# Moving the row-maximum reductions on VectorE and the loop boundary on TensorE in a masked graph attention kernel

## What is computed

```
xn = layernorm(x)
q, k, v = xn @ Wq, xn @ Wk, xn @ Wv            # 2 heads of 64
scores = (q * SCALE) @ k.T, -9e15 where adj == 0
attn = softmax(scores)
sat = attn @ v
out = concat(sat[:2048] @ weightr, sat[2048:] @ weightd) + bias
x = x + leaky_relu(out)
y = layernorm(x); the two best of 8 experts by y @ Wg + bg
x = x + sum over chosen experts of (gelu(y @ W1 + b1) @ W2 + b2)
```

## Time and profile before

| | |
|---|---|
| median of 3 runs | 804.45 us (804.39 to 804.54) |
| profiled execution | 804.59 us, its span 802.9 us |
| granted TensorE clock | 0.999 of full |
| busy: TensorE / its weight loads | 776.4 us (97%) / 576.5 us (72%) |
| busy: VectorE | 650.5 us (81%) |
| busy: ScalarE | 684.7 us (85%) |
| busy: GpSimd | 683.3 us (85%) |
| chain that ended last | PE 84%, POOL 5%, DVE 5%, issue 4% |
| L692, mask preparation, 64 times | 676 / 824 / 1725 ns (least, median, most) |
| L743, row maximum, 64 times | 156 / 157 / 158 ns |

### The profile page before, as it was taken

How to read it: one execution, slowest core, us unless ns; L and a number is a source line. 1 busy time by engine, 2 the same in 40 slices (tenths; PEclk the granted TensorE clock), 3 DMA queues, 4 the chain that set the end, 5 groups by cost and what they waited for, 6 DMA issues and landing times.

```text
span 802.9 us, 34579 instructions
## 1 busy us (share of the span) xinstructions
PE 776.4 (97%) x13088; PEld 576.5 (72%) x13088; DVE 650.5 (81%) x1470; ACT 684.7 (85%) x1099; POOL 683.3 (85%) x673
## 2 busy tenths in 40 slices
PE   4999999999999999999999999999998999999997
PEld 2467777777777777777777777777777677777775
DVE  7887999889889898989889888988985777545554
ACT  4678888888889888888888888888988999999996
POOL 4799999999999999999999999999986767667664
PEclk9999999999999999999999999999999999999999
DMA  9633533353344334343443335334200000000000
GB/s 230 119 61 61 86 64 66 61 85 59 59 64 79 59 65 68 63 72 59 70 73 61 63 61 85 59 59 65 53 1 2 2 14 16 15 15 13 13 13 13
DMA packets 40906, 45.02 MB, mean 56 GB/s; under 512 B 22168, under 2 KB 32160, under 8 KB 40864
## 3 DMA queue, kind: packets, MB, share of 16 engines
q0 software_dynamic: 9216, 33.56, 25.8%
q1 hardware_dynamic: 31216, 10.71, 5.7%
q10 hardware_dynamic: 432, 0.20, 0.1%
HBM read 71.72 MB, written 2.10 MB: 92 GB/s over the span
## 4 chain that ended last, share of the span: by engine, by line
PE 84%; POOL 5%; DVE 5%; issue 4%; ACT 1%; DMA 1%; DVEq 0%; POOLq 0%
PE ps L1074 18%; PE ps L1095 18%; PE ps L1128 13%; PE ps L1121 10%; PE ps L1253 4%; PE ps L1255 3%; PE ps L1254 3%; PE ps L1196 3%; PE ps L1197 3%; PE ps L1198 3%; PE ps L1139 2%; POOL w_pair L367 1%; DVE prob L735 1%; POOL pt_half L351 1%; PE ps L1147 1%
## 5 line engine op out<-in xcount | busy, mean ns | idle before, releaser
L735 DVE CUSTOM_DVE_ANT_0 prob<-ps,mask 128x1024 f32<-128x1024 f32 x256 | 310.5, 1219 | 40.9 <-PE ps L1074 38.8
L351 POOL TENSOR_TENSOR pt_half<-pt_raw,pt_half 128x512 f16<-128x512 f32 x252 | 302.8, 1222 | 10.5
L534 ACT ACTIVATE prob<-prob,nmax 128x1024 f32<-128x1024 f32 x256 | 292.9, 1144 | 0.1
L1095 PEld LDWEIGHTS ps<-ident,prob 64*128 64x128 f32 x4096 | 154.1, 138 | 66.1 <-issue 62.4
L1074 PE MATMUL ps<-k_half,q_row 64*128 64x512 f16 x1536 | 188.2, 376 | 1.2 <-DVE k_half L685 0.8
L1095 PE MATMUL ps<-ident,prob 64*128 64x64 f32 x4096 | 180.9, 227 | 6.8 <-ACT prob L534 2.0
L461 POOL TENSOR_TENSOR prob<-prob 128x512 f16<-128x512 f32 x104 | 123.8, 1194 | 56.9 <-ACT prob L612 53.9
L347 POOL TENSOR_SCALAR pt_half<-pt_raw 128x1024 f16<-128x1024 f32 x126 | 138.6, 1100 | 22.4 <-PE ps L1121 11.8
L1128 PE MATMUL ps<-pt,v_sb 128*64 128x128 f32 x2048 | 125.9, 276 | 0.0
L967 DVE SCALAR_TENSOR_TENSOR x_sb<-ps,k_half,x_sb 128x128 f32<-128x128 f32 (+1 forms) x256 | 72.1, 344 | 64.6 <-PE ps L1255 61.9
L1074 PEld LDWEIGHTS ps<-k_half,q_row 64*128 64x128 f16 x1536 | 73.8, 95 | 61.0 <-issue 9.7
(11 more groups left out here) (124 smaller groups left out, 1115.5 us busy)
## 6 DMA issues: line engine op xcount, KB each, us to landing
mask<-in_adj POOLq DMA_DIRECT2D x64, 512.0 KB, 5.4
q_row<-q_nat SPq DMA_DIRECT2D x128, 32.0 KB, 1.9
x_sb<-in_x SPq DMA_DIRECT2D x4, 512.0 KB, 7.0
out<-x_sb SPq DMA_DIRECT2D x8, 256.0 KB, 2.3
x2t_hi<-in_L_ffn_W SPq DMA_DIRECT2D x1, 1024.0 KB, 6.5
wq_sb<-in_L_gnn_Wq ACTq DMA_DIRECT2D x1, 64.0 KB, 2.8
wk_sb<-in_L_gnn_Wk ACTq DMA_DIRECT2D x1, 64.0 KB, 4.4
wv_sb<-in_L_gnn_Wv ACTq DMA_DIRECT2D x1, 64.0 KB, 5.6
```

Of the source, the lines that this page charges most:

```text
L351: ins = pool.tensor_tensor(pt_lo[:, q, part, :], pt_raw[:, q % 2, part, :], pt_hi[:, q, part, :], ALU.subtract)
L534: act.activation(prob[:, h, cols], prob[:, h, cols], ACT.Exp, bias=nmax[:, h:h + 1], scale=-1.0, accum_out=sums[:, j, h, p:p + 1]).then_in ...
L735: dve.tensor_tensor_reduce(out=prob[:, h, col_of(p)], in0=ps[:, 2 * (u % 2):2 * (u % 2) + 2, :].rearrange("p b c -> p (b c)"), in1=mask[:, ...
L1095: ins = pe.transpose(ps[:, bank + half, t * DH:(t + 1) * DH], prob[part, h, (p * KT + t) * P:(p * KT + t + 1) * P], ident[part, part])
```

## The change

The row maximum of head 0 is issued behind the mask preparation of unit 5, not ahead of it. The row maximum of head 1 leaves the end of its step: it is issued in the next step, behind the copy of unit 0 and ahead of the masking of unit 0. Tile 0 keeps its own place for it. On TensorE block 0 of step 4 is written out, the loop runs 13 times instead of 14 over blocks 1 to 3 of an even step, the odd step and block 0 of the next even step, and blocks 1 to 3 of step 30 and step 31 are written out behind it.

```diff
--- before.py
+++ after.py
@@ -42,6 +42,7 @@
 BOTH_HEADS = (2, 3, 6, 7)
 AV_BLOCK = 2
 LOOP_UNIT = 2
+LOOP_BLOCK = 1
 SPLIT_P = (1, 3)
 SPLIT_UNITS = (1, 3, 5, 7)
 NS = len(SPLIT_UNITS)
@@ -876,12 +877,16 @@
                         finish_tile(i - 2, par)
                     if prior and u in DVE_COPIES:
                         copy_pt(i - 1, u, early, last)
+                    if prior and u == 0 and not early:
+                        row_max(i - 1, 1, 7)
                     if now:
                         mask_scores(i, par, u, prior)
-                        if u in (5, 7):
-                            row_max(i, u // 7, u)
                     if ahead and u in (1, 5):
                         make_mask(i + 1, 1 - par, u // 4)
+                    if now and u == 5:
+                        row_max(i, 0, 5)
+                    if now and u == 7 and not prior:
+                        row_max(i, 1, 7)
                     if post and par == 1:
                         if u == 1:
                             invert_sums(i - 3)
@@ -1158,9 +1163,10 @@
                     ins = pe.matmul(scores_t, x2t_lo[:, rows], wg_pair[:, 0, :], start=False, stop=True)
                 ins.then_inc(logit_psum, PAIR)
 
-            def step(i, par, prior=True, now=True, drain=True, post=True, ready=True, early=False):
-
-                for k in range(NU // 2):
+            def step(i, par, prior=True, now=True, drain=True, post=True, ready=True, early=False,
+                     blocks=range(NU // 2)):
+
+                for k in blocks:
                     if prior:
                         transposes(i - 1, 2 * k, early, not now)
                     if now:
@@ -1203,7 +1209,13 @@
             step(2, 0, post=False)
             pe.wait_ge(small_split, SMALL_SPLITS)
             step(3, 1, ready=False)
-            pairs(pe, 4, NT, step)
+            step(4, 0, blocks=range(LOOP_BLOCK))
+            with pe.Fori(0, (NT - 4) // 2 - 1) as k:
+                step(2 * k + 4, 0, blocks=range(LOOP_BLOCK, NU // 2))
+                step(2 * k + 5, 1)
+                step(2 * k + 6, 0, blocks=range(LOOP_BLOCK))
+            step(NT - 2, 0, blocks=range(LOOP_BLOCK, NU // 2))
+            step(NT - 1, 1)
             step(NT, 0, now=False)
             attend(NT - 1, NP - 2)
             x2_transpose(NT - 2 * PAIR)
```

## The result

The changed kernel takes 800.74 us, the median of 6 runs (800.33 to 801.28), against 804.5 us of the kernel before (6 runs, 804.29 to 805.06). The ratio is 0.9948, its 95% interval 0.9938 to 0.9958. So it is faster by 3.8 us, where 7.9 were forecast, and 0.5 us outside the range of 794.8 to 800.2. The profiled execution took 801.28 us, at a granted clock of 0.999.

The account below looks back on a forecast made before the run. TensorE, busy 97%, was taken as the bound. Gaps of 0.24 + 0.18 + 0.22 + 0.04 = 0.68 us over twelve pairs give 8.2, plus about 0.3, less 0.4: net 8.1, so 796.6 us, range 794.8 to 800.2.

Parts of the forecast that it names:

- Rivals A and B: A: port stays lost, 0.22 us gaps stay, 799.2, 10%; B: block 0 comes back only by half, 799.1, 11%.
- Rival D: Slower: unit 2's transposes wait for ScalarE's late copy of unit 1 in every row; 808.3 with no cover, 5%.
- part 3: TensorE's loop turned by one block: ahead of the even step 0.04 us comes back and 0.07 stays.
- the three other gaps: Block 0 of even and odd steps, and ahead of the odd step: 0.24, 0.18 and 0.22 us to come back.
- the fourth gap: TensorE's gap ahead of the even step, 0.11 us over: 0.04 us to come back, 0.07 to stay.
- part 1: Head 1's maximum moved: block 0 regains 0.24 and 0.18 us; ScalarE's unit 1 copy ends at about its old time.
- Rival E: No change: GpSimd becomes the period, its 0.91 us idle against 0.68 a pair asked back; about 804.5, 5%.
- The range: Forecast time between 794.8 (all 0.75 us a pair back) and 800.2 us, taking in rivals at 799.1 to 799.3.
- the sum: Twelve pairs at 0.68 us, 8.2 us; about 0.3 from smaller earlier gaps, less 0.4 in the last step; net 8.1.
- The branch: TensorE's loop branch, 208 ns, hidden behind the fp32 attention at its new place: 0.04 us a pair back.
- Rival C: The branch is exposed at its new place behind the fp32 attention: 2.7 us less gain, 799.3, 4%.
- The last step: No scores fill TensorE there; unit 2's exp starts 0.4 us later, charged in full, once.

Follow-up runs that it names:

- e5: Kernel before with the leaky ReLU moved from unit 5 of the odd step to unit 1 of the next even step; 802.54 us.
- e1: Kernel before with only head 1's row maximum moved behind the next row's first copy; 801.49 us.
- e2: Kernel before with only head 0's row maximum moved behind the mask preparation; 803.76 us.
- e6: Kernel before with one 128x256 memset (0.3 us) added on GpSimd in every even step; 807.67 us.
- e3: Kernel before with only TensorE's loop turned by one block; 807.48 us.
- e4: Changed kernel with TensorE's loop as it was before, so both row maxima moved and no turn; 800.39 us.
- e7: Kernel before with both row maxima moved and the leaky ReLU moved to unit 1 of the next even step, loop not turned; 796.19 us.
- e9: Changed kernel, turned loop included, with the leaky ReLU moved to unit 1 of the next even step; 797.4 us.
- e11: Changed kernel with the leaky ReLU moved to unit 1 of the next even step and the last tile's head 1 maximum ahead of unit 0's copy; 796.84 us.
- e10: Changed kernel with one 128x256 memset added on GpSimd in every even step; 804.5 us.

## Why the prediction was wrong

**Right.** Where the losses were and what ended three of them. Block 0 gave 0.24 us in the even and 0.19 in the odd step, at the times worked out. The preparation of unit 5 won the port and took 0.76 us, the gap behind it closed. Rivals A and B fell with that. Not each gap was the maximum's own: the even step's block 0 also closes without moving it (e5), the odd one's by either maximum (e1, e2).

**Right, and without cost to TensorE.** The exp of unit 2 waits for its maximum, 10.1 us in all, and TensorE never waits for ScalarE's copy of unit 1 in the loop. Rival D fell.

**Wrong: the step that failed** stands in part 3: "The rest of that gap, 0.07 us, belongs to VectorE's copy of 314.13, which hangs on the division chain of the odd step, untouched here. So 0.04 us comes back and 0.07 stays." The copy hangs on more than the division: that chain's last instruction, the leaky ReLU, ends 0.28 us after a subtraction of GpSimd's. GpSimd was not moved by the 0.63 us that the three other gaps gave back. From its splitting of unit 7 to its subtractions of unit 5 it took 0.34 us less, and only by that did the copy come earlier. The difference went into the fourth gap: 0.24 + 0.19 + 0.20 closed and 0.29 opened, 0.34 in all. The sum over the loop is 13 × 0.34 = 4.4 us in place of 8.8 by the same count.

**What the 0.34 us are** can be read from the earlier trace rows and the timeline above. From the splitting of unit 7 to that of unit 1 nothing was gained (4.23 and 4.25), because ScalarE's copy of unit 1, behind the late exp, came at its old time. This stood in part 1 as harmless, and on a ring it is not. Then the splitting of unit 1 took 0.31 less, that of unit 5 0.29 more, and its subtractions 0.33 less (2.29 in place of 2.62).

**Rival E** was nearest, GpSimd as the period, at 5% and at the wrong price. It set 0.91 us of idle time against 0.68 asked back and took the rest for room. That idle time was part of the ring, and e6 shows that it was no room.

**The range** was too narrow for this, and its lower end doesn't follow from its own count: 12 pairs at 0.75 us, with the 0.3 and the 0.4 us of the sum, give 795.6 and not 794.8.

**The branch**: 0.04 us a pair was forecast and nothing came back, since the copy ended that gap with or without it (e3, e4). With the ring cut it is 0.12 (e7 against e9). Rival C had it exposed in each pass, and no pass shows that. "The unrolled code is longer by two steps, fetched in sequence: 0" failed in some executions: in e3, e9 and e11 TensorE stalls for 1.8 to 2.7 us in all, in the first pass only. The Trainium skill, "Runtime: NRT & Kernel Launch", Instruction fetch mechanics, names such a stall for a taken branch; here it lies within the first pass, before TensorE has taken the loop's branch. In all three a fetch of instructions had come late, 10.5 to 11.1 us after the one ahead of it, where the changed kernel's took 6.4; the changed kernel's profile has no such stall. Why the fetch is late stays open.

**The last step**: 0.4 us was charged, and step 30 to the experts took 0.25 more (51.00 against 50.75); e11 takes 0.30 less than e9. Timelines of the changed kernel in the last step:

```profile
597.88 1.15 ACT L535 ACTIVATE prob<-prob,nmax 128x1024 f32<-128x1024 f32 x1 [0.23 <-DVE nmax L744]
...
601.31 0.71 PE L1100 MATMUL ps<-ident,prob 64*128 64x64 f32 x16 [1.23 <-ACT prob L535]
```

The exp waits for its maximum, and TensorE idles 1.23 us before the third transposes against 0.87. In e11 it is 0.73.

## What to carry to other kernels

Before counting small gaps together, ask for the one that was not touched what its releaser waits for, and follow it once round the loop: if it comes back to itself through another engine, the period is that ring's length and closed gaps elsewhere reappear in it. Idle time within such a ring is not slack; a short dummy instruction on the idle engine, with and without the suspected link, tells the two apart at the price of two runs. And when a gain is half of what was forecast while every closed gap is closed, look for the gap that has grown.

## What the runs showed of the hardware that I had not expected

A two-input VectorE instruction of 256 elements a row ended 0.28 us after GpSimd's instruction each time, whether it was recorded with 0.69, 1.03 or, in e7, 1.26 us: the duration tells when it was issued, the end tells who held it. Who wins is decided by some tenths: the same splitting took 1.05 to 1.49 us and the same preparation 0.69 to 1.72.

The first pass over a turned loop stalled TensorE for 1.81, 2.67 and (0.86 + 1.26) us in three of five profiled executions of kernels with it (e10's and the changed kernel's own are free of it). In e9 the granted clock was 0.54 of full in the 3.4 us behind the 2.67 us stall; behind e3's 1.81 us it stayed full. The runs of e9 spread over 4.9 us, those of e7 lie within 0.6.
